# Self attention of a decoder layer on one core: the causal cut of the transposed scores, made by TensorE or by GpSimd

## The chip, the core and the metric

The kernel runs on one core of a Trainium2 chip. The time is that of the whole kernel on the device, in microseconds (us), median of several runs; smaller is better. TensorE (PE) multiplies, with its weight loads listed apart as PEld; VectorE is DVE, ScalarE is ACT, GpSimd is POOL, SyncE (SP) issues the transfers. Each engine works through its own program in order, and the programs meet in semaphores.

## The reference, cut to what matters

One decoder layer on x (4 x 1024 x 512) with a context (4 x 1024 x 512), 16 heads of 32: layer norm and self attention, layer norm and cross attention, layer norm and a two-layer MLP of 2048, each added to its input. Of the self attention:

```python
scores = jnp.einsum('bhqd,bhkd->bhqk', q, kh) / jnp.sqrt(jnp.float32(D))
block_repr = k.reshape(B, nb, BLOCK, D).mean(axis=2)
r = jax.nn.relu(block_repr @ r_w1.T + r_b1) @ r_w2.T + r_b2
keep0 = jax.nn.sigmoid(r[0, :, 0]) > 0.5
allowed = keep0[:, None] & keep0[None, :]
...
scores = jnp.where(allowed_pos[None, None], scores, NEG)
causal = jnp.triu(jnp.ones((S, S), bool), k=1)
scores = jnp.where(causal[None, None], -jnp.inf, scores)
p = jax.nn.softmax(scores, axis=-1)
out = jnp.einsum('bhqk,bhkd->bhqd', p, vh)
```

Every query sees only keys up to its own place, and blocks of 64 keys or queries that a small router drops are pushed to -1e9. All outputs are f32.

## The kernel before, in words

The layer is a chain of stages, each with its own buffers: projections of the context (tag `d_`) and of x (`a_`), self attention (`b_`), projection (`c_`), cross attention (`e_`), projection (`f_`), MLP (`m_`). Self and cross attention are the same function, `attention_stage`; `causal` is true in `b_` alone, and only that stage is touched.

A round n is one group of four heads (HG = 4) of one batch: 16 rounds. In a round the transposed scores (keys down the partitions, queries along the columns) are worked through in twelve steps: k = 0 to 3 for the first half of the 512-query halves (`h` = 0) with key tiles t = 0 to 3, and k = 4 to 11 for the second with t = 0 to 7. `first` is the first query column of a step that any key of its tile may reach: 0, 128, 256, 384 for k = 0 to 3, 0 for k = 4 to 8, then 128, 256, 384 for k = 9 to 11. A step is diagonal when its key tile lies among the queries of its half: k = 0 to 3 and 8 to 11.

TensorE's program (from L1148): in step k, head by head, the scores of step k + 1 (`scores`, L1093, into one of three PSUM banks), matmuls of the scores in their natural layout for the row maxima of the next rounds (`max_scores`, L1063), spread over the steps by a planner (L790 to L820) that counts for each step how much VectorE has to do (`busy`); after head 2 the values' matmuls of step k (`weigh`, L1111), and at the steps named by `sum_at` the sums of a half (`sum_up`, L1122). In `scores` each f32 score matmul of a diagonal step is followed by a second one, of a bf16 identity with `mask_kq`, that adds -1e30 above the diagonal in the first 128 valid columns (L1107). The natural scores have such a mask of their own (L1085).

ScalarE takes the exp of each head's scores into `probs` (L1049), of which there are NF + NR = 5 + 5 buffers of 4 x 512 columns: five in turn for the first step of each group, five for the others. The softmax sums are not taken per step: GpSimd adds the probs of a group's later steps onto those of its first (`add`, L930), and `sum_up` multiplies ones with the first's probs only. `groups` (L757) has three groups: (0, 4), (4, 4), (8, 4), as (first step, number of steps). The add onto a first step waits until `weigh` has read it (L936), since it overwrites it. VectorE copies the values' result out (`copy_outs`, L963) and turns and inverts the sums (`invert`, L987), one or more steps after their cause; GpSimd multiplies both (`normalise`, L942). All these places are counted from `last_step` and `sum_at` (L763).

Of the kernel before, what the change touches and what calls it, by code (L numbers as in the profile page):

```python
# [29 lines left out]
ALU = mybir.AluOpType  # L30
# [6 lines left out]
P = 128  # L37
B, S, D = 4, 1024, 512
H, DH = 16, 32
HG = P // DH  # L40
# [4 lines left out]
TOK = 512  # L45
SUB = TOK // P
HALVES = S // TOK
# [8 lines left out]
ROWS = AUG + 3  # L56
# [684 lines left out]
def attention_stage(nc, tag, ident, q_hi, q_lo, k_hi, k_lo, v, out, keep=None, mask_qk=None,  # L741
                    mask_kq=None, ident_bf=None):
    causal = keep is not None
    N = B * NG
# [4 lines left out]
             for t in range((h + 1) * TOK // P if causal else KT)]  # L749
# [6 lines left out]

    groups = ([(0, 4), (4, 4), (8, 4)] if causal else  # L757
              [(0, 3), (3, 3), (6, 2), (8, 3), (11, 3), (14, 2)])
# [3 lines left out]
    firsts_of = {h: [k for k in firsts if steps[k][0] == h] for h in range(HALVES)}  # L762
    sum_at = {h: last_step[h] + 3 for h in range(HALVES)}  # L763
    VISIT_HEAD = 2
# [28 lines left out]
    for h in range(HALVES):  # L793
        busy[(last_step[h] + 1) % NS] += 0.7
        busy[(sum_at[h] + 1) % NS] += 1.7
# [26 lines left out]
    with ExitStack() as ctx:  # L822
# [18 lines left out]
        consts_set, ones_set = sem("consts_set"), sem("ones_set")  # L841
        added = sem("added")
        loaded = [sem(f"loaded{p}") for p in range(SETS)]
# [11 lines left out]
        with nc.Block() as block:  # L855
# [64 lines left out]
            def _(pool):  # L920
# [7 lines left out]
                pool.wait_ge(consts_set, FILLS * (SETS - 1))  # L928

                def add(n, k):  # L930
                    k0, _ = groups[group_of[k]]
                    before = n * len(rests) + rests.index(k)
                    first = steps[k][2]
                    pool.wait_ge(exped, n * NBLOCKS + (k + 1) * HG)
                    if k == k0 + 1:
                        pool.wait_ge(weighed, n * NS + k0 + 1)  # L936
                    else:
                        pool.wait_ge(added, before)
                    into = probs[:, home(n, k0), :, first:TOK]
                    pool.tensor_tensor(into, into, probs[:, home(n, k), :, first:TOK], ALU.add).then_inc(added, 1)  # L940
# [6 lines left out]
                for n in range(N):  # L947
                    for k in range(NS):
                        for h in range(HALVES):
                            back, at = divmod(sum_at[h] + 3, NS)  # L950
                            if at == k and n >= back:
                                normalise(n - back, h)
                        if k in rests:
                            add(n, k)
# [3 lines left out]
            def _(dve):  # L958
# [47 lines left out]
                for n in range(N):  # L1006
                    for k in range(NS):
                        for h in range(HALVES):
                            back, at = divmod(last_step[h] + 1, NS)
                            if at == k and n >= back:  # L1010
                                copy_outs(n - back, h)
                            back, at = divmod(sum_at[h] + 1, NS)
                            if at == k and n >= back:
                                invert(n - back, h)
# [38 lines left out]
            def _(pe):  # L1053
# [9 lines left out]
                def max_scores(n, u):  # L1063
# [14 lines left out]
                    for bank in range(banks):  # L1078
                        cols = max(width, 256)
                        diagonal = causal and bank == banks - 1  # L1080
                        last = pe.matmul(nat[:, bank_of[u] + bank, 0:cols], qs[p][0:rows, j, t * P:(t + 1) * P],  # L1081
                                         ks[p][0:rows, j, bank * width:bank * width + cols], start=True,
                                         stop=not diagonal)
                        if diagonal:
                            last = pe.matmul(nat[:, bank_of[u] + bank, width - P:width], ident_bf[:], mask_qk[:],  # L1085
                                             start=False, stop=True)
# [6 lines left out]
                def scores(n, k, j):  # L1093
# [3 lines left out]
                    if k == 0 and j == 0:  # L1097
# [3 lines left out]
                    lo = min(first, TOK - 256)  # L1101
                    diagonal = causal and t * P >= h * TOK
                    last = pe.matmul(st_ps[:, bank, lo:TOK], ks[p][0:ROWS, j, t * P:(t + 1) * P],  # L1103
                                     qs[p][0:ROWS, j, h * TOK + lo:(h + 1) * TOK], start=True,
                                     stop=not diagonal)
                    if diagonal:
                        last = pe.matmul(st_ps[:, bank, first:first + P], ident_bf[:], mask_kq[:],  # L1107
                                         start=False, stop=True)
                    last.then_inc(st_ready, 1)

                def weigh(n, k):  # L1111
                    h, t, first = steps[k]
                    pe.wait_ge(exped, n * NBLOCKS + (k + 1) * HG)
                    if t == 0 and n * HALVES + h >= 1:
                        pe.wait_ge(outs_copied, n * HALVES + h)
# [32 lines left out]
                for n in range(N):  # L1148
                    for k in range(NS):
                        for j in range(HG):  # L1150
# [12 lines left out]
                            if j == VISIT_HEAD:  # L1163
                                weigh(n, k)
                                for h in range(HALVES):
                                    back, at = divmod(sum_at[h], NS)
                                    if at == k and n >= back:
                                        sum_up(n - back, h)
                sum_up(N - 1, HALVES - 1)
        sem.clear()  # L1170
# [322 lines left out]
```

## Time and profile before

| | |
|---|---|
| Median of 3 runs | 3414.98 us (3411.88 to 3415.19) |
| Profiled execution | 3417.59 us, span 3415.8 us |
| Mean granted TensorE clock in it | 0.953 |
| TensorE busy | 3130.5 us (92%), 16138 matmuls |
| PEld / VectorE / ScalarE / GpSimd busy | 60% / 52% / 36% / 57% |
| TENSOR_REDUCE of row maxima, L975, `b_` | x512, 364.7 us busy |
| ACTIVATE exp, L1049, `b_` | x768, 350.4 us busy |
| TENSOR_TENSOR adds, L940, `b_` | x144, 446.8 us busy |
| Score matmuls, L1103, `b_` | x768, 299.1 us busy |

The profile is of one execution, by the hardware profiler. Busy is the union of an engine's instructions; matmuls overlap, and their ends are modelled, so the distance from one start to the next says more than a duration. "Idle before, releaser" is how long the engine stood still before an instruction and what ended that. The chain that ended last lies in the MLP stage, since each stage begins when the one before is over; a stage's own time is therefore read from its own stretch.

### The profile page before, as it was taken

The numbers are of one execution on the slowest core, as the hardware profiler recorded it, in microseconds if no ns is written. First come the engines' busy times: TensorE is split into PE (matmuls) and PEld (weight loads), VectorE is DVE, ScalarE is ACT, GpSimd is POOL, SyncE is SP. The second block draws the span as 40 slices with busy tenths as digits, with TensorE's granted clock in tenths as the row PEclk, the third lists the DMA queues.
The fourth block names the chain that finished last, engine by engine and source line by source line (L and its number), as shares of the span: only waits on it lengthen the run. The fifth ranks groups of instructions, "written<-read, shape, count | busy, mean of one in ns | idle before, by whom it ended". The sixth has DMA issues, their size and how long they took to land. (4 is left out here: it accounts for less than half of the span.)

```text
span 3415.8 us, 41706 instructions
## 1 busy us (share of the span) xinstructions
PE 3130.5 (92%) x16138; PEld 2036.1 (60%) x16138; DVE 1772.4 (52%) x2373; ACT 1228.9 (36%) x2305; POOL 1943.8 (57%) x896
## 2 busy tenths in 40 slices
PE   7978997999999986978999999999967599999999
PEld 6867885455555545754444444444346488888887
DVE  4526554666666635758777777777449311111110
ACT  2112220455555552222666666666622211111111
POOL 3114333677777776644888888888866443222232
PEclk9979997999999998996999999999988799999999
DMA  5535546444444405535242424242047521111110
GB/s 203 174 123 173 197 148 162 93 100 100 100 100 100 100 17 179 206 140 129 59 91 59 91 58 92 57 93 54 10 140 282 206 74 50 50 50 50 50 47 15
DMA packets 211604, 360.66 MB, mean 106 GB/s; under 512 B 16312, under 2 KB 92600, under 8 KB 207312
## 3 DMA queue, kind: packets, MB, share of 16 engines
q1 hardware_dynamic: 211408, 358.01, 36.5%
q8 instruction: 127, 2.08, 0.3%
q14 instruction: 69, 0.57, 0.1%
HBM read 214.20 MB, written 142.61 MB: 104 GB/s over the span
## 5 line engine op out<-in xcount | busy, mean ns | idle before, releaser
L940 POOL TENSOR_TENSOR e_probs<-e_probs 128x2048 f32<-128x2048 f32 x160 | 733.4, 4585 | 173.1 <-ACT e_probs L1049 168.4
L1049 ACT ACTIVATE e_probs<-e_st 128x512 f32<-128x512 f32 x1024 | 554.2, 598 | 404.0 <-PE e_st L1103 394.1
L975 DVE TENSOR_REDUCE e_neg_max<-e_nat 128x1 f32<-128x1024 f32 x512 | 602.1, 1218 | 146.3 <-PE e_nat L1081 141.3
L940 POOL TENSOR_TENSOR b_probs<-b_probs 128x1536 f32<-128x1536 f32 (+1 forms) x144 | 446.8, 3103 | 224.3 <-ACT b_probs L1049 214.5
L1049 ACT ACTIVATE b_probs<-b_st 128x512 f32<-128x512 f32 (+3 forms) x768 | 350.4, 490 | 386.2 <-PE b_st L1107 298.3
L975 DVE TENSOR_REDUCE b_neg_max<-b_nat 128x1 f32<-128x128 f32 (+7 forms) x512 | 364.7, 751 | 181.2 <-PE b_nat L1085 178.6
L1301 POOL TENSOR_TENSOR m_hid_lo<-m_hid,m_hid_hi 128x512 fp32r<-128x512 f32 x128 | 165.2, 1290 | 463.2 <-DVE m_hid_hi L1322 463.2
L1103 PE MATMUL e_st<-e_qs,e_ks 99*128 99x512 f32 x1024 | 387.1, 428 | 4.3 <-ACT e_probs L1049 2.9
L1081 PE MATMUL e_nat<-e_ks,e_qs 96*128 96x512 f32 x1024 | 343.2, 424 | 39.5 <-DVE e_neg_max L975 27.9
L1322 DVE CAST m_hid_hi<-m_hid 128x512 fp32r<-128x512 f32 x128 | 58.5, 457 | 600.4 <-ACT m_hid L1274 600.4
L1103 PEld LDWEIGHTS e_st<-e_qs,e_ks 99*128 99x128 f32 x1024 | 174.2, 188 | 257.3 <-ACT e_probs L1049 201.1
L1103 PE MATMUL b_st<-b_qs,b_ks 99*128 99x512 f32 (+2 forms) x768 | 299.1, 432 | 5.0 <-DVE b_turned_sums L994 2.5
L1274 ACT ACTIVATE m_hid<-m_h_ps,m_b 128x512 f32<-128x512 f32 x128 | 88.2, 689 | 593.3 <-PE m_h_ps L113 593.3
L1081 PE MATMUL b_nat<-b_ks,b_qs 97*128 97x384 f32 (+4 forms) x768 | 251.0, 409 | 27.8 <-DMA b_ks<-b_key_mask 19.1
L1117 PE MATMUL e_pv<-e_probs,e_vs 128*32 128x512 f32 x2048 | 273.3, 606 | 0.7 <-ACT e_probs L1049 0.7
L1081 PEld LDWEIGHTS e_nat<-e_ks,e_qs 96*128 96x128 f32 x1024 | 194.5, 199 | 124.6 <-DVE e_neg_max L975 66.2
L1103 PEld LDWEIGHTS b_st<-b_qs,b_ks 99*128 99x128 f32 x768 | 147.5, 199 | 141.2 <-ACT b_probs L1049 89.7
L113 PE MATMUL m_h_ps<-m_x_hi,m_w_hi 128*128 128x512 f32 x512 | 200.9, 392 | 22.2 <-DMA m_x_lo<-xt_lo 20.6
L113 PE MATMUL m_o_ps<-m_w_hi,m_hid_hi 128*128 128x512 f32 x512 | 203.2, 397 | 2.2 <-POOL m_hid_lo L1301 2.2
L113 PE MATMUL m_o_ps<-m_w_hi,m_hid_lo 128*128 128x512 f32 x512 | 203.1, 397 | 0.0
L113 PE MATMUL m_o_ps<-m_w_lo,m_hid_hi 128*128 128x512 f32 x512 | 203.1, 397 | 0.0
L113 PE MATMUL m_h_ps<-m_x_hi,m_w_lo 128*128 128x512 f32 x512 | 201.3, 393 | 0.0
(197 smaller groups left out, 5313.2 us busy)
## 6 DMA issues: line engine op xcount, KB each, us to landing
b_qs<-sq_hi SPq DMA_DIRECT2D x30, 512.0 KB, 6.6
b_ks<-sk_hi SPq DMA_DIRECT2D x30, 512.0 KB, 14.1
e_qs<-cq_hi SPq DMA_DIRECT2D x30, 512.0 KB, 6.7
e_ks<-ck_hi SPq DMA_DIRECT2D x30, 512.0 KB, 14.4
d_x<-in_ctx SPq DMA_DIRECT2D x8, 1024.0 KB, 6.1
ck_hi<-d_part_hi SPq DMA_DIRECT2D x32, 256.0 KB, 6.2
ck_lo<-d_part_lo SPq DMA_DIRECT2D x32, 256.0 KB, 6.1
cv<-d_tok_out SPq DMA_DIRECT2D x32, 256.0 KB, 5.1
```

The source lines that it names most:

```text
L113: last = pe.matmul(out, w, x, start=(start and n == 0 and m == 0), stop=(stop and n == len(pairs) - 1 and m == 2))
L940: pool.tensor_tensor(into, into, probs[:, home(n, k), :, first:TOK], ALU.add).then_inc(added, 1)
L975: dve.tensor_reduce(neg_max[:, u:u + 1], nat[:, bank_of[u]:bank_of[u] + banks, 0:keys // banks], AX.XY, ALU.max, negate=True).then_inc(max ...
L1049: act.activation(probs[:, home(n, k), j, first:TOK], st_ps[:, bank_at("scores", blk), first:TOK], ACT.Exp).then_inc(exped, 1)
L1081: last = pe.matmul(nat[:, bank_of[u] + bank, 0:cols], qs[p][0:rows, j, t * P:(t + 1) * P], ks[p][0:rows, j, bank * width:bank * width + co ...
L1103: last = pe.matmul(st_ps[:, bank, lo:TOK], ks[p][0:ROWS, j, t * P:(t + 1) * P], qs[p][0:ROWS, j, h * TOK + lo:(h + 1) * TOK], start=True, ...
L1117: last = pe.matmul(pv_ps[j * DH:(j + 1) * DH, first:TOK], vs[n % SETS][:, t, j * DH:(j + 1) * DH], probs[:, home(n, k), j, first:TOK], sta ...
L1274: act.activation(hid[:, c % RING, :], h_ps[:, c % RING, :], ACT.Relu, bias=b1_sb[:, c:c + 1]).then_inc(relu_done, 1)
L1301: pool.tensor_tensor(hid_lo[:, c % RING, :], hid[:, c % RING, :], hid_hi[:, c % RING, :].bitcast(F32), ALU.subtract).then_inc(hid_lo_done, 1)
L1322: dve.tensor_copy(hid_hi[:, c % RING, :], hid[:, c % RING, :]).then_inc(hid_hi_done, 1)
```

## The change

Only `attention_stage` is touched, and for cross attention nothing changes. In self attention

- `scores` issues no mask matmul; the score matmul ends its bank alone;
- GpSimd's new `clear(n, k)` runs an `affine_select` in place on the 128 diagonal columns of the four heads' probs of each diagonal step, once the exps of the step are there, and writes 0 where the key lies behind the query; it counts up `cleared`;
- `weigh` and `add` wait for `cleared` on diagonal steps;
- `weigh` is issued a step later (`LATE = 1`), and what is counted from it with it: `sum_at`, `copy_outs`, `invert`, `normalise`, and the planner's `busy`; the last weighing of the stage stands behind the loop;
- group (4, 4) becomes (4, 2) and (6, 2): step 6 is a first step, so its probs are not added onto others, and the sums of the second half run over three groups of four matmuls.

The natural scores keep their masks. The rest is a change of a name.

```diff
--- before.py
+++ after.py
@@ -754,13 +754,16 @@
 
 
 
-    groups = ([(0, 4), (4, 4), (8, 4)] if causal else
+    groups = ([(0, 4), (4, 2), (6, 2), (8, 4)] if causal else
               [(0, 3), (3, 3), (6, 2), (8, 3), (11, 3), (14, 2)])
     firsts = [k for k, _ in groups]
     rests = [k for k in range(NS) if k not in firsts]
     group_of = [max(g for g, k0 in enumerate(firsts) if k0 <= k) for k in range(NS)]
     firsts_of = {h: [k for k in firsts if steps[k][0] == h] for h in range(HALVES)}
-    sum_at = {h: last_step[h] + 3 for h in range(HALVES)}
+
+    LATE = 1 if causal else 0
+    diagonal = [causal and t * P >= h * TOK for h, t, _ in steps]
+    sum_at = {h: last_step[h] + LATE + 3 for h in range(HALVES)}
     VISIT_HEAD = 2
 
 
@@ -791,7 +794,7 @@
     busy = [0.0] * NS
     busy[TURN] += 0.6
     for h in range(HALVES):
-        busy[(last_step[h] + 1) % NS] += 0.7
+        busy[(last_step[h] + LATE + 1) % NS] += 0.7
         busy[(sum_at[h] + 1) % NS] += 1.7
     free = []
     for at in range(NBLOCKS):
@@ -839,7 +842,7 @@
         pv_ps = ctx.enter_context(nc.psum_tensor(tag + "pv", [P, 512], F32))
 
         consts_set, ones_set = sem("consts_set"), sem("ones_set")
-        added = sem("added")
+        added, cleared = sem("added"), sem("cleared")
         loaded = [sem(f"loaded{p}") for p in range(SETS)]
         rows_loaded = [sem(f"rows_loaded{p}") for p in range(SETS)]
         nat_ready, maxed, max_turned, max_split = sem("nat_ready"), sem("maxed"), sem("max_turned"), sem("max_split")
@@ -927,11 +930,19 @@
                     pool.memset(qs[p][AUG:ROWS].bitcast(F32), 0.0).then_inc(consts_set, 1)
                 pool.wait_ge(consts_set, FILLS * (SETS - 1))
 
+                def clear(n, k):
+                    cut = probs[:, home(n, k), :, steps[k][2]:steps[k][2] + P]
+                    pool.wait_ge(exped, n * NBLOCKS + (k + 1) * HG)
+                    pool.affine_select(out=cut, in_=cut, compare_op=ALU.is_ge, fill=0.0, base=0,
+                                       pattern=[[0, HG], [1, P]], channel_multiplier=-1).then_inc(cleared, 1)
+
                 def add(n, k):
                     k0, _ = groups[group_of[k]]
                     before = n * len(rests) + rests.index(k)
                     first = steps[k][2]
                     pool.wait_ge(exped, n * NBLOCKS + (k + 1) * HG)
+                    if diagonal[k]:
+                        pool.wait_ge(cleared, n * sum(diagonal) + sum(diagonal[:k + 1]))
                     if k == k0 + 1:
                         pool.wait_ge(weighed, n * NS + k0 + 1)
                     else:
@@ -950,6 +961,8 @@
                             back, at = divmod(sum_at[h] + 3, NS)
                             if at == k and n >= back:
                                 normalise(n - back, h)
+                        if diagonal[k]:
+                            clear(n, k)
                         if k in rests:
                             add(n, k)
                 normalise(N - 1, HALVES - 1)
@@ -1006,7 +1019,7 @@
                 for n in range(N):
                     for k in range(NS):
                         for h in range(HALVES):
-                            back, at = divmod(last_step[h] + 1, NS)
+                            back, at = divmod(last_step[h] + LATE + 1, NS)
                             if at == k and n >= back:
                                 copy_outs(n - back, h)
                             back, at = divmod(sum_at[h] + 1, NS)
@@ -1077,11 +1090,11 @@
                         pe.wait_ge(maxed, n * UNITS + u + 1 - reach[u])
                     for bank in range(banks):
                         cols = max(width, 256)
-                        diagonal = causal and bank == banks - 1
+                        cut = causal and bank == banks - 1
                         last = pe.matmul(nat[:, bank_of[u] + bank, 0:cols], qs[p][0:rows, j, t * P:(t + 1) * P],
                                          ks[p][0:rows, j, bank * width:bank * width + cols], start=True,
-                                         stop=not diagonal)
-                        if diagonal:
+                                         stop=not cut)
+                        if cut:
                             last = pe.matmul(nat[:, bank_of[u] + bank, width - P:width], ident_bf[:], mask_qk[:],
                                              start=False, stop=True)
                     last.then_inc(nat_ready, 1)
@@ -1099,18 +1112,15 @@
                     bank_free("scores", blk)
                     bank = bank_at("scores", blk)
                     lo = min(first, TOK - 256)
-                    diagonal = causal and t * P >= h * TOK
-                    last = pe.matmul(st_ps[:, bank, lo:TOK], ks[p][0:ROWS, j, t * P:(t + 1) * P],
-                                     qs[p][0:ROWS, j, h * TOK + lo:(h + 1) * TOK], start=True,
-                                     stop=not diagonal)
-                    if diagonal:
-                        last = pe.matmul(st_ps[:, bank, first:first + P], ident_bf[:], mask_kq[:],
-                                         start=False, stop=True)
-                    last.then_inc(st_ready, 1)
+                    pe.matmul(st_ps[:, bank, lo:TOK], ks[p][0:ROWS, j, t * P:(t + 1) * P],
+                              qs[p][0:ROWS, j, h * TOK + lo:(h + 1) * TOK], start=True,
+                              stop=True).then_inc(st_ready, 1)
 
                 def weigh(n, k):
                     h, t, first = steps[k]
                     pe.wait_ge(exped, n * NBLOCKS + (k + 1) * HG)
+                    if diagonal[k]:
+                        pe.wait_ge(cleared, n * sum(diagonal) + sum(diagonal[:k + 1]))
                     if t == 0 and n * HALVES + h >= 1:
                         pe.wait_ge(outs_copied, n * HALVES + h)
                     for j in range(HG):
@@ -1161,11 +1171,14 @@
                                 for u in later_units[k][j]:
                                     max_scores(n + 2, u)
                             if j == VISIT_HEAD:
-                                weigh(n, k)
+                                if n * NS + k >= LATE:
+                                    weigh(*divmod(n * NS + k - LATE, NS))
                                 for h in range(HALVES):
                                     back, at = divmod(sum_at[h], NS)
                                     if at == k and n >= back:
                                         sum_up(n - back, h)
+                for k in range(NS - LATE, NS):
+                    weigh(N - 1, k)
                 sum_up(N - 1, HALVES - 1)
         sem.clear()
```

## Rows read from the trace of the kernel before

**Rows 1.** Busy time of each engine in stretches of self attention (instructions in brackets).

```profile
core 0: us, PE busy (x) PEld busy (x) DVE busy (x) ACT busy (x) POOL busy (x), PEclk, DMA share, GB/s
1030.00:1115.00 85.00, 81.97 (x563) 42.79 (x562) 55.73 (x85) 43.80 (x97) 60.85 (x22) 1.00 0.46 100
775.00:860.00 85.00, 81.61 (x560) 42.53 (x559) 55.71 (x84) 43.24 (x96) 60.85 (x22) 1.00 0.46 100
901.35:943.92 42.57, 41.05 (x283) 21.44 (x282) 27.94 (x43) 21.97 (x49) 30.43 (x12) 1.00 0.47 100
```

**Rows 2.** Timeline, TensorE at the stage's end: start, length, instruction, count.

```profile
1281.69 3.64 PE L1129 MATMUL b_st<-b_probs,b_ones 128*32 128x512 f32 x16 [6.79 <-POOL b_probs L940]
```

**Rows 3.** Timeline, TensorE: score matmuls with masks, then the values'.

```profile
900.83 0.23 PE L1107 MATMUL b_st<-mask_kq,ident_bf 128*128 128x128 bf16 x1
900.87 0.48 PE L1103 MATMUL b_st<-b_qs,b_ks 99*128 99x512 f32 x1
901.19 0.23 PE L1107 MATMUL b_st<-mask_kq,ident_bf 128*128 128x128 bf16 x1
901.35 0.43 PE L1117 MATMUL b_pv<-b_probs,b_vs 128*32 128x128 f32 x8
```

**Rows 4.** Timeline, TensorE: f32 matmuls behind an f32 matmul and behind a mask.

```profile
917.35 0.48 PE L1103 MATMUL b_st<-b_qs,b_ks 99*128 99x512 f32 x1
917.76 1.06 PE L1117 MATMUL b_pv<-b_probs,b_vs 128*32 128x512 f32 x8
918.76 0.73 PE L1103 MATMUL b_st<-b_qs,b_ks 99*128 99x512 f32 x2
919.32 0.28 PE L1081 MATMUL b_nat<-b_ks,b_qs 97*128 97x256 f32 x1
919.45 0.23 PE L1085 MATMUL b_nat<-mask_qk,ident_bf 128*128 128x128 bf16 x1
919.49 0.36 PE L1081 MATMUL b_nat<-b_ks,b_qs 97*128 97x256 f32 x1
919.69 0.23 PE L1085 MATMUL b_nat<-mask_qk,ident_bf 128*128 128x128 bf16 x1
```

**Rows 5.** Timeline, TensorE: the two sums of a round, and a wait behind one.

```profile
911.75 1.90 PE L1129 MATMUL b_st<-b_probs,b_ones 128*32 128x512 f32 x16
913.58 0.39 PE L1103 MATMUL b_st<-b_qs,b_ks 99*128 99x256 f32 x1
...
913.85 0.47 PE L1103 MATMUL b_st<-b_qs,b_ks 99*128 99x512 f32 x1
914.49 0.73 PE L1103 MATMUL b_st<-b_qs,b_ks 99*128 99x512 f32 x2 [0.17 <-DVE b_turned_sums L994]
...
926.57 1.04 PE L1129 MATMUL b_st<-b_probs,b_ones 128*32 128x512 f32 x8
927.54 0.73 PE L1103 MATMUL b_st<-b_qs,b_ks 99*128 99x512 f32 x2
```

**Rows 6.** Groups of GpSimd's instructions: count, busy us, mean ns, idle before.

```profile
L940 POOL TENSOR_TENSOR b_probs<-b_probs 128x2048 f32<-128x2048 f32 x48 | 219.5, 4572 | 51.6 <-ACT b_probs L1049 47.0
L940 POOL TENSOR_TENSOR b_probs<-b_probs 128x1536 f32<-128x1536 f32 x32 | 110.5, 3454 | 146.6 <-ACT b_probs L1049 146.6
L945 POOL TENSOR_TENSOR b_outs<-b_outs,b_turned_sums 128x512 f32<-128x512 f32 x32 | 41.3, 1291 | 5.6 <-DVE b_turned_sums L998 5.6
L926 POOL MEMSET b_ks<- 3x4096 f32 x2 | 7.0, 3508 | 0.0
```

**Rows 7.** Timeline, GpSimd at the kernel's start: two of its four selects.

```profile
1.60 0.29 POOL L1407 TENSOR_SCALAR_AFFINE_SELECT ident<-ident 128x128 f32<-128x128 f32 x1 [0.25 <-POOL mask_kq L1404]
1.85 0.29 POOL L1407 TENSOR_SCALAR_AFFINE_SELECT ident_bf<-ident_bf 128x128 bf16<-128x128 bf16 x1
```

**Rows 8.** Timeline, TensorE: values' matmuls of steps 1, 3, 8, 9 and 11.

```profile
908.48 0.85 PE L1117 MATMUL b_pv<-b_probs,b_vs 128*32 128x384 f32 x8
915.15 0.43 PE L1117 MATMUL b_pv<-b_probs,b_vs 128*32 128x128 f32 x8
934.50 1.06 PE L1117 MATMUL b_pv<-b_probs,b_vs 128*32 128x512 f32 x8
938.38 0.85 PE L1117 MATMUL b_pv<-b_probs,b_vs 128*32 128x384 f32 x8
943.92 0.42 PE L1117 MATMUL b_pv<-b_probs,b_vs 128*32 128x128 f32 x8
```

**Rows 9.** Timeline, TensorE: the longest wait of a round.

```profile
938.17 0.28 PE L1091 MATMUL b_nat<-ident,b_neg_max 128*32 128x128 f32 x1 [0.83 <-DVE b_neg_max L975]
```

## What the change should do to the time, worked out before it was run

> **What bounds the kernel now.** I read the busy time of each engine by stretches first. Of the change only the self attention stage is touched: in the steady part of its loop TensorE is busy 81.6 to 82.0 of 85 us at the full granted clock, while GpSimd is busy 60.9, VectorE 55.7 and ScalarE 43 to 44 [rows 1]. One round (one group of four heads, twelve steps of four heads) takes 42.57 us, and TensorE works in 41.05 of them. So TensorE's own program order sets the time, and what counts is the distance from the start of one matmul to the start of the next. Two things must be asked: how much of that distance goes away, and which instruction of TensorE then waits for GpSimd. In the last round there are no row maxima left to work out, and there GpSimd is the bound: the last group sums wait 6.79 us for it [rows 2].
>
> **The sums on TensorE, per round.** A score matmul is followed by its mask matmul on the eight diagonal steps (k = 0 to 3 and 8 to 11), four heads each: 32 masks a round, 512 in all. I read starts. The mask itself holds the next matmul up by only 0.04 us (900.83 to 900.87), but the matmul after a mask starts its successor later than it would after another f32 matmul: 256 columns take 0.13 us after an f32 matmul (919.32 to 919.45) and 0.20 after a mask (919.49 to 919.69) [rows 3, 4]. A removed mask with an f32 matmul behind it thus saves 0.04 + 0.07 = 0.11 to 0.12 us. Before the values' matmuls, score and mask take 0.32 + 0.16 = 0.48 us, a score alone 0.41 (917.35 to 917.76) [rows 3, 4]: 0.07 saved. 24 of the first kind and 8 of the second give 24 x 0.115 + 8 x 0.07 = 3.3 us.
>
> The fourth group of sums adds four f32 matmuls of 512 columns side by side, once a round: two groups take 1.83 us, one 0.97 [rows 5], so 0.86 more. The sums of the second half move from step 2 to step 3 of the next round, away from where a score now waits for the transpose that frees their bank (0.17 us idle; start to start 0.64 instead of 0.34): 0.3 back. Nothing else of TensorE's order is new: the values' matmuls are the same, one step later, behind the same number of scores. Without any new wait a round saves 3.3 - 0.86 + 0.3 = 2.8 us.
>
> **GpSimd, per round.** Gone is the add of step 6, 4.57 us [rows 6]. New are eight clears of 128 x (4 x 128). The load is no trouble: 30.4 us now [rows 1], about 31.5 then. The price C of a clear is not in the trace. The nearest rows are the four selects of 128 x 128 at the start of the kernel: 0.29 us each, starts 0.25 apart [rows 7]. Low end: their 0.25 and for 384 more elements the slope of a memset (4096 elements in 3.51 us, 0.86 ns an element) [rows 6]: 0.25 + 0.33 = 0.58 us. High end: four times 0.295, 1.18 us; the two-input operation of 512 elements takes 1.29 [rows 6]. I take 0.70, near the low end, because the select reads one operand as the memset row does in writing, and the two-input row pays for a second. The Trainium skill, GPSIMD Engine Reference, section Performance pitfalls for Q7 kernels, has compare-then-select bodies at 2.03 cycles an element, and 1.03 when unrolled twice; at its 1.2 GHz that would be an estimate of 0.87 or 0.44 us for 512 elements before the fixed part, and the total below would be about 2 or 13 us less than before; no row here says which body the select has.
>
> **The new wait.** The weighing of step k (the values' matmuls) waits for the clear of k. GpSimd works in order, and ahead of some clears stands an add that itself can only start when the weighing of the group's first step is over, since the add writes on those probabilities (L936). With the weighing a step later that release comes a step later too. I number TensorE's places by the step at which they stand; the weighing at place p is that of step p - 1.
>
> Place 9 to 11: at place 9 the values of step 8 are weighed, 1.0 us; about 0.1 us later the add of step 9 starts, 3.45 us, then the normalising product that now stands at step 10, 1.29, then the clear of step 10: 5.84 + C after place 9. TensorE needs the clear at place 11. Place 9 to 11 takes 943.92 - 938.38 = 5.54 us now [rows 8]; 0.4 more since two wider weighings stand between, 0.8 less for the eight masks in it: 5.1. The stall is 0.7 + C, 1.4 us with C = 0.70.
>
> Place 1 to 3: the weighing of step 0, then the add of step 1 and the clear of step 2: 1.0 + 0.1 + 3.45 + C = 4.55 + C. TensorE takes 915.15 - 908.48 = 6.67 us now [rows 8]; less 1.83 for the sums that move behind place 3 and 0.3 for the wait behind them [rows 5], less 0.5 for five masks, 0.5 more for wider weighings, and about 0.5 more for one row maximum that the planner moves from step 4 to step 3 (its sum_at entry moves): 5.0. The stall is C - 0.4, 0.3 us. The clears of steps 3, 8, 9, 11 and 0, by the same count, come before they are needed, that of step 11 by under half a microsecond.
>
> What else moves stays covered. The first-of-group probs take four of five buffers a round instead of three; the exp of step 6 now waits for the sums of the second half of the round before, which stand two steps (some 8 us) ahead of it; without that cover ScalarE, and behind it the scores, would stand still for what is missing. SyncE's load of the round after next waits for the last weighing of the round before, a step later, and has most of a round left. The copy, the inverse and the normalising product each move by a step along with what they wait for.
>
> What waits behind a stalled weighing is all of TensorE's queue: scores, row maxima, and through them ScalarE and VectorE; nothing of it is got back, since TensorE is the bound. Where it stands still for 0.83 us in each round already, its granted clock stays at 1.00 [rows 1, 9], the 2.4 GHz level; I expect that with 1.4 too.
>
> **The sum.** A round: 2.8 - 1.4 - 0.3 = 1.1 us saved, or in general 2.5 - 2C. Fourteen rounds have all their row maxima: 15 us. At the ends some comes back: the values' matmuls begin one step late (2 us), the last two rounds hang on GpSimd rather than on the masks (eight clears against one add, 8 x 0.7 - 4.57 = 1 us, with the adds waiting for later weighings another 2), and the third group in the last sums runs at the lower clock, where two take 3.64 us against 1.90 in mid-stage [rows 2, 5]: some 1 us beyond the masks' saving there. Together 6. Result: 9 us less. On the profiled run (3417.6 us, span 3415.8) that is 3408.6, on the median of the runs shown 3415.0 - 9 = 3406 us, which is what I forecast. With C = 0.58 it is 3402, with C = 0.80 3409; gain and loss balance at C near 1.04.
>
> **The rivals.**
> Slow clears: at C = 1.18 the two stalls leave 14 x 0.14 = 2 us of gain, 6 us at the ends are lost, and the clears of steps 11 and 0 come late as well, since their slack of some 0.4 us is gone, by up to 0.9 a round: 3419 to 3432. It decides from C = 1.04. For it: four separate runs of 128 elements in each partition. Against it: the 0.25 us of 128 must hold some fixed part. Chance 0.24, a third of it within 0.2%.
> The mask is only its 0.04: if the f32 score behind a removed mask keeps its 0.20, a round saves 1.3 - 0.86 + 0.3 = 0.7 and stalls about 1.1 (TensorE arrives later): 0.4 lost a round, 6 at the ends, 3427. Against it stand the two 256-column rows of [rows 4]. Chance 0.08.
> No stalls: if GpSimd is at place 11 in time, a round keeps 2.8 and the kernel ends near 3415 - 39 + 6 = 3382. Against it: the order of GpSimd's program and the 3.45 us row. Chance 0.05.
> The forecast itself has 0.63: 0.41 of it lies beyond 0.2%, and 0.22 within (C from 0.80 to 1.04, or masks worth a little less).
>
> **Chances and range.** 0.2%, 6.8 us, is about what a measurement tells here. Faster 0.41 + 0.05 = 0.46; same 0.22 + 0.08 = 0.30; slower 0.16 + 0.08 = 0.24. The range goes from 3392 (C = 0.58, masks worth a bit more, cheap ends) to 3430.
>
> **What would show it.** In the profile after, no matmul writes scores from the mask; score matmuls of 256 columns stand 0.13 us apart where nothing holds them; TensorE waits for the clears 14 to 16 times for about 1.4 us each before the 256-column weighing at place 11 and shorter before that at place 3; clears last 0.6 to 0.8 us; the sums of the second half take 2.7 us. A round is 41.3 to 41.6 us long. The forecast falls if clears last over a microsecond, if the stalls sit elsewhere, or if the granted clock dips within a round.

## The result and the profile after

The changed kernel takes 3450.2 us, median of four runs (3441.0 to 3459.4), against 3415.1 us before (3411.9 to 3415.4): 1.0105 of the time, 95% interval 1.0075 to 1.0135. I had forecast 3406 us, range 3392 to 3430. It became slower by 35 us where I expected 9 us less. The profiled execution is the slowest of the four, 3459.4 us with a span of 3457.7; the time before scatters over 3.5 us, that after over 18.

The first view, the busy time by stretches, already holds the answer. These rows of after stand against [rows 1]; columns as there.

```profile
core 0: us, PE busy (x) PEld busy (x) DVE busy (x) ACT busy (x) POOL busy (x), PEclk, DMA share, GB/s
600.00:1290.00 690.00, 641.32 (x3858) 325.82 (x3860) 412.53 (x622) 331.59 (x736) 464.44 (x274) 0.88 0.39 86
...
818.25:863.64 45.39, 42.41 (x258) 21.75 (x258) 27.84 (x42) 21.77 (x48) 30.61 (x18) 0.89 0.43 94
863.64:913.46 49.82, 46.96 (x257) 23.49 (x257) 27.93 (x42) 21.80 (x48) 30.59 (x18) 0.79 0.39 86
1000.94:1042.65 41.71, 38.06 (x257) 19.41 (x258) 27.28 (x42) 21.75 (x48) 30.67 (x18) 1.00 0.46 102
1042.65:1084.38 41.73, 38.09 (x257) 19.42 (x257) 27.28 (x42) 21.76 (x48) 30.66 (x18) 1.00 0.46 102
```

The last four stretches are one round each, from one matmul that turns the row maxima (now L1104) to the next. All four hold the same work: 257 or 258 matmuls, 48 exps, 18 operations of GpSimd. Two have a granted clock of 1.00 and take 41.7 us, 0.85 less than the 42.57 before; two have 0.89 and 0.79 and take 45.4 and 49.8. From 600 to 1290 us the granted clock is 0.88; before it was 0.98 there, below 1.00 only at the two ends of the loop.

What TensorE does where the clock falls, and where it does not (timeline of after; start, length, instruction, idle before and its releaser):

```profile
1049.57 0.64 PE L1127 MATMUL b_pv<-b_probs,b_vs 128*32 128x256 f32 x8 [1.58 <-POOL b_probs L936]
1050.14 0.68 PE L1115 MATMUL b_st<-b_qs,b_ks 99*128 99x512 f32 x2
...
870.56 0.99 PE L1127 MATMUL b_pv<-b_probs,b_vs 128*32 128x256 f32 x8 [1.58 <-POOL b_probs L936]
871.48 1.12 PE L1115 MATMUL b_st<-b_qs,b_ks 99*128 99x512 f32 x2
872.39 0.84 PE L1094 MATMUL b_nat<-b_ks,b_qs 97*128 97x384 f32 x2
873.04 0.33 PE L1098 MATMUL b_nat<-mask_qk,ident_bf 128*128 128x128 bf16 x1
...
913.46 0.28 PE L1104 MATMUL b_nat<-ident,b_neg_max 128*32 128x128 f32 x1 [1.01 <-DVE b_neg_max L988]
```

Both weighings are those of step 10 at place 11. Both waited 1.58 us for the clear (L936). Behind the first a pair of 512-column scores takes 0.68 us, behind the second 1.12: from there TensorE runs at its lower level, 1.2 GHz, for 10 to 20 us. Such a fall comes in 11 of the 15 round-to-round distances of the profiled run, each time within 2 us behind the end of this wait (ten waits of 1.58 us and one of 1.34). In the other four the wait was 0.76, 1.05 and twice 1.58 us: it can pass without a fall. Some 6 us earlier TensorE waits 1.01 us for the last row maximum, 0.83 before [rows 9]; it waits 1.01 us also where only the masks are gone (e8 below).

GpSimd and its new instruction, in a round at the full clock (timeline of after):

```profile
1044.14 3.47 POOL L951 TENSOR_TENSOR b_probs<-b_probs 128x1536 f32<-128x1536 f32 x1 [1.75 <-PE b_pv L1127]
1047.56 1.28 POOL L956 TENSOR_TENSOR b_outs<-b_outs,b_turned_sums 128x512 f32<-128x512 f32 x1
1048.77 0.65 POOL L936 TENSOR_SCALAR_AFFINE_SELECT b_probs<-b_probs 128x512 f32<-128x512 f32 x1
```

All its clears between 600 and 1300 us (group of instructions; columns as in [rows 6]):

```profile
L936 POOL TENSOR_SCALAR_AFFINE_SELECT b_probs<-b_probs 128x512 f32<-128x512 f32 x124 | 78.4, 639 | 56.2 <-ACT b_probs L1062 55.8
```

This is the chain that I had worked out for place 11: the add of step 9, released by the weighing of step 8, the normalising product, the clear. The clear takes 0.64 us.

The other stall, at place 3, is one for which the profile names the wrong releaser (timeline of after):

```profile
1015.07 3.47 POOL L951 TENSOR_TENSOR b_probs<-b_probs 128x1536 f32<-128x1536 f32 x1 [1.51 <-PE b_pv L1127]
1018.50 0.63 POOL L936 TENSOR_SCALAR_AFFINE_SELECT b_probs<-b_probs 128x512 f32<-128x512 f32 x1
...
1019.28 0.64 PE L1127 MATMUL b_pv<-b_probs,b_vs 128*32 128x256 f32 x8 [0.49 <-ACT b_probs L1062]
```

The exps of that step are older; the clear ends at 1019.13, and 0.15 us later the weighing starts, the same distance as at place 11 (1049.42 to 1049.57). Without clears this wait is not there (e3 below).

### The profile page after: what moved, and what is told of

It reads as the page before. It is cut to its first block and busy times, and to the rows that moved or that the text cites. A ratio compares the mean times of both kernels' runs of the same rounds, so it can differ in the third digit from the quotient of the medians.

```text
span 3457.7 us, 41149 instructions
## 1 busy us (share of the span) xinstructions
PE 3148.6 (91%) x15754; PEld 2036.2 (59%) x15754; DVE 1772.4 (51%) x2373; ACT 1224.5 (35%) x2305; POOL 1946.9 (56%) x1008
## 5 line engine op out<-in xcount | busy, mean ns | idle before, releaser
L951 POOL TENSOR_TENSOR b_probs<-b_probs 128x1536 f32<-128x1536 f32 (+3 forms) x128 | 374.3, 2924 | 205.2 <-PE b_pv L1127 196.1
L1314 POOL TENSOR_TENSOR m_hid_lo<-m_hid,m_hid_hi 128x512 fp32r<-128x512 f32 x128 | 165.1, 1290 | 463.4 <-DVE m_hid_hi L1335 463.4
L1094 PE MATMUL b_nat<-b_ks,b_qs 97*128 97x384 f32 (+4 forms) x768 | 260.2, 424 | 25.0 <-DMA b_ks<-b_key_mask 19.2
L1127 PE MATMUL b_pv<-b_probs,b_vs 128*32 128x512 f32 (+3 forms) x1536 | 184.0, 554 | 33.5 <-POOL b_probs L936 30.4
```

The lines of the kernel that those rows point to most:

```text
L1127: last = pe.matmul(pv_ps[j * DH:(j + 1) * DH, first:TOK], vs[n % SETS][:, t, j * DH:(j + 1) * DH], probs[:, home(n, k), j, first:TOK], sta ...
L1314: pool.tensor_tensor(hid_lo[:, c % RING, :], hid[:, c % RING, :], hid_hi[:, c % RING, :].bitcast(F32), ALU.subtract).then_inc(hid_lo_done, 1)
```

## The experiments

Two theories for the lower clock. A: it falls because TensorE stands still for the clear, as long as it does. B: it falls because the mask matmuls' work is gone from TensorE. Rounds are counted from one turning matmul to the next, in the profiled run of each kernel. A "fall" is a stretch at 1.2 GHz that begins within these fifteen distances. The low stretch in which every loop starts is not counted: it ends between 604 and 631 us, why so differently is not shown, and the first distance is 40 to 50 us long. Where rounds are given, the first is left out.

**e1, the normalising product a step earlier.**

```diff
-                            back, at = divmod(sum_at[h] + 3, NS)
+                            back, at = divmod(sum_at[h] + 2, NS)
```

> The changed kernel with one edit: GpSimd's normalising product is issued a step earlier, so that at step 10 it no longer stands between the add of step 9 and the clear of step 10. All results are computed. In the changed kernel rounds at the full clock last 41.7 us and rounds with a fall of the granted clock 45 to 50. Theory A, the clock falls because TensorE stands still (1.0 to 1.6 us for the clear of step 10, shortly after 1.0 us for the row maxima): that stall shrinks by 1.29 us to about 0.1, the clock holds, rounds take about 40.5 us and the kernel about 3385. Theory B, the clock falls because the mask matmuls' work is gone from TensorE: the clock falls as often as before, some rounds still take over 44 us, and the kernel takes 3420 to 3440.

Measured: 3392.3 us (3388.7 to 3395.3), 0.9923 of before (0.9907 to 0.9939). Rounds of 40.5 us, all alike after the first, no fall. Busy time in a stretch of it, and its weighing at place 11:

```profile
1030.00:1115.00 85.00, 79.92 (x536) 40.61 (x535) 57.65 (x87) 45.73 (x100) 65.42 (x37) 1.00 0.49 107
```

```profile
1089.82 0.64 PE L1127 MATMUL b_pv<-b_probs,b_vs 128*32 128x256 f32 x8 [0.36 <-POOL b_probs L936]
```

The wait at place 11 went from 1.58 to 0.36 us, and the clock is at 1.00. One number is changed in the source, and 58 us lie between the two medians: 1.2 us a round is the shorter wait, 18 us in 15 rounds, and some 40 are left for the clock. For A, against B.

**e2, every clear ahead of the add of the step before.**

```diff
                         if diagonal[k]:
                             clear(n, k)
-                        if k in rests:
-                            add(n, k)
+                        m, i = divmod(n * NS + k - 1, NS)
+                        if m >= 0 and i in rests:
+                            add(m, i)
+                add(N - 1, NS - 1)
                 normalise(N - 1, HALVES - 1)
```

> The changed kernel with the adds issued one step later in GpSimd's program, so that each clear stands ahead of the add of the step before it and behind no add that waits for a weighing. All results are computed. Theory A: no weighing waits for a clear, the clock holds at 1.00 in the steady part, rounds take 39.5 to 40.0 us, the kernel 3372 to 3382. Theory B: no stall either, but the clock still falls in most rounds, and the kernel takes 3410 to 3430.

Measured: 3375.5 us (3374.5 to 3380.7), 0.9878 (0.9859 to 0.9897). Rounds of 39.5 us (two of 39.9 and 40.2), no fall. TensorE's waits between 700 and 1190 us, summed (us, times, longest):

```profile
PE b_nat L1106 <- DVE b_neg_max L990: 12.2, 12, 1.0
PE b_nat L1096 <- DVE b_neg_max L990: 6.7, 25, 0.3
PE b_st L1117 <- DMA b_qs<-b_max_lo: 0.4, 1, 0.4
```

No weighing waits any more. The adds did not need to go first: GpSimd has time for both.

**e3, no clears and no waits for them.** The edit takes `clear`'s call and the two waits on `cleared` out of the changed kernel.

> The changed kernel without the clears and without the waits for them; probabilities above the diagonal stay in, so this part of the computation is left out. It shows what the masks' removal, the late weighing and the fourth group give together with GpSimd out of the way: rounds of 39.5 to 39.9 us at the full clock (42.57 less 2.8) by both theories. Theory A: the clock holds, about 3370 to 3378. Theory B: it falls in most rounds, over 3400.

Measured: 3376.2 us (two runs, 3372.3 and 3380.2), 0.9876 (0.9851 to 0.9902); rounds of 39.5 us, apart from a few of up to 40.1, no fall. This kernel leaves the causal cut of the transposed scores out, so it serves as a measure only. With e2 it says that well-placed clears cost nothing that these runs could show, and that the masks may go without the clock falling: B is out.

**e4, masks back and a stall as before.**

```diff
+                    done = n * sum(diagonal) + sum(diagonal[:k])
+                    if done:
+                        pool.wait_ge(filled, done)
+                    pool.memset(filler[:], 0.0).then_inc(filled, 1)
                     pool.affine_select(out=cut, in_=cut, compare_op=ALU.is_ge, fill=0.0, base=0,
...
+                    if diagonal[k]:
+                        last = pe.matmul(st_ps[:, bank, first:first + P], ident_bf[:], mask_kq[:],
+                                         start=False, stop=True)
```

> The changed kernel with the mask matmuls put back after the scores (the clears then change nothing), and a memset of 760 elements to a spare buffer ahead of every clear, about 0.7 us each, so that the weighing at place 11 still waits more than 1 us for its clear. All results are computed. Full-clock rounds should take about 44.5 us by both theories (42.57, 0.9 for the fourth group, 1.3 to 1.9 of stalls, less 0.3 to 0.6 for the later weighing). Theory A: the clock falls as in the changed kernel, in half of the rounds or more, over 3475. Theory B: the masks keep TensorE active enough, the clock holds, 3450 to 3465.

Measured: 3516.8 us (two runs, 3498.2 and 3535.4), 1.029 (1.022 to 1.035). Rounds without a fall take 44.8 us, seven of fifteen have one and take 48.9 to 53.0. The wait at place 11 is 1.35 to 1.37 us in all rounds but the first, with a fall behind it or without. The weighing at place 11, and the busy time of a stretch:

```profile
1071.62 0.64 PE L1136 MATMUL b_pv<-b_probs,b_vs 128*32 128x256 f32 x8 [1.35 <-POOL b_probs L941]
```

```profile
1115.00:1200.00 85.00, 80.14 (x519) 42.20 (x522) 49.66 (x76) 39.99 (x87) 64.26 (x47) 0.92 0.46 101
```

All masks are back and the clock falls, with a wait of 1.35 us at place 11. With e1 to e3 the question between A and B is closed.

**e5, e2 with the three old groups.**

```diff
-    groups = ([(0, 4), (4, 2), (6, 2), (8, 4)] if causal else
+    groups = ([(0, 4), (4, 4), (8, 4)] if causal else
```

> The kernel of e2_clears_first with the three groups of the kernel before: GpSimd adds step 6 again (4.58 us a round) and TensorE sums two groups in the second half instead of three. All results are computed. e2 took rounds of 39.5 us, GpSimd busy 32.7 of 42.5. If TensorE alone sets the time there, the round loses the fourth group's 0.86 us: 38.6 to 38.8, the kernel 3360 to 3366. If GpSimd, then busy about 36 of 38.7 us with adds that wait for weighings, gets in the way, weighings wait for clears again, the clock may fall, and it takes 3375 or more.

Measured: 3363.9 us (3361.7 to 3373.8), 0.9847 (0.9827 to 0.9868), the fastest of all. Rounds of 38.6 to 38.7 us, no fall. Busy time in a stretch:

```profile
1030.00:1115.00 85.00, 81.86 (x561) 41.63 (x560) 59.18 (x92) 47.52 (x107) 77.00 (x44) 1.00 0.55 120
```

GpSimd is busy 77.0 of 85 us, and still TensorE hardly waits for it: between 700 and 1190 us its listed waits for ScalarE sum to 2.4 us, and none for GpSimd is listed. Once the clears stand first, the fourth group relieves an engine that does not need it. The round is 0.88 us shorter without it.

**e6 and e7, the parts that keep the masks.** e6 is the kernel before with `LATE = 1` alone; e7 is e6 with the fourth group.

> The kernel before with the weighing, and what is counted from it, one step later, and nothing else of the change: masks on TensorE, three groups, no clears. All results are computed. My sum gave the later sums 0.3 us a round, since a score no longer waits for the transpose behind them: rounds of 42.0 to 42.3 us, 3405 to 3413. A rival: the later weighing costs as much elsewhere, 3415 to 3420.

Measured: 3404.8 us (3404.5 to 3405.7), 0.9958 (0.9944 to 0.9973), rounds of 41.9 us.

> The kernel of e6 with the fourth group of sums: masks on TensorE, no clears. All results are computed. The step from e6 is the group's price: 0.86 us a round and 1 us more at the cold end, 15 us in all, so 3420 to 3428. The step from here to e3_no_clears (3376) is then the 512 masks: at 0.115 and 0.07 us each 53 us; at 0.04 each it would have been 20.

Measured: 3416.5 us (ten runs, 3412.7 to 3422.7), 0.9989 (0.9978 to 1.0000), rounds of 42.7 us. So the later weighing gives 0.70 us a round (42.57 to 41.87), over twice my figure, and the fourth group costs 0.87 a round and 12 us in all. From here to e3 the masks go: 42.74 to 39.53, 3.2 us a round. The two medians lie 40 us apart, less than fifteen times 3.2 and than the 53 that I expected; 4.8 us of that is the first distance of e3's profiled run, 49.6 us against 44.8, with its longer low stretch.

**e8, the masks off alone.** The kernel before without the second matmul in `scores`.

> The kernel before without the mask matmuls of the transposed scores and nothing put in their place: probabilities above the diagonal stay in, that part of the computation is left out. If a mask costs 0.115 us where an f32 matmul follows and 0.07 ahead of the values, rounds take 42.57 - 3.3 = 39.2 to 39.4 us at a granted clock of 1.00 and the kernel 3365 to 3372. If it costs only its own 0.04, 41.3 us and 3395. Were TensorE's clock to fall for want of the masks' work, rounds of over 42 us would appear.

Measured: 3375.5 us (two runs, 3375.3 and 3375.7), 0.9872 (0.9853 to 0.9892), rounds of 39.8 us, no fall in them. That is less than I expected of it: 2.8 us a round and not 3.3, 0.4 less than between e7 and e3: in this kernel a score still waits for the transpose behind the sums (3.5 us in 12 times). This kernel too leaves the cut out. The price of a removed mask lies at 0.09 to 0.10 us, far from the 0.04 of the rival.

**e9 and e11, a stall elsewhere.** Both are e2 with a wait of TensorE for the add of step 5, in a stretch of 512-column matmuls: in e9 behind the weighing at step 6, in e11 ahead of it.

```diff
+                                if causal and k == 6:
+                                    pe.wait_ge(added, n * len(rests) + rests.index(5) + 1)
```

> The kernel of e2_clears_first with one wait more: behind the weighing at step 6, TensorE waits until GpSimd has done the add of step 5. By the trace that is about 1.0 us of standstill, as long as the wait for the clear of step 10 in the changed kernel, but seven to eight us after the last narrow step, in the stretch of 512-column matmuls. All results are computed. Theory A1, any standstill of about 1 us in a round lets the granted clock fall: falls in half of the rounds or more, as in the changed kernel, 3420 or more. Theory A2, it takes the wait where it stood, behind 1.0 us of waiting for row maxima and among the narrow steps: the clock holds, rounds take 40.5 to 40.7 us, the kernel 3390 to 3396.

Measured: 3391.3 us (two runs, 3388.9 and 3393.8), 0.9927 (0.9898 to 0.9956). Rounds of 40.1 to 40.3, no fall. But the stall was 0.58 us, not 1.0, so it could not tell the places apart; hence e11, where `weigh` holds the same wait for k = 5:

> The kernel of e9 with its extra wait ahead of the weighing at step 6 instead of behind it. In e9 TensorE stood still for 0.58 us there and the clock held; the weighing of 1.0 us in front filled the rest. Now the standstill should be 1.5 to 1.6 us, the same as at place 11 in the changed kernel (1.58), but 512-column matmuls stand on both sides. All results are computed. Theory A1, a standstill of 1.6 us lets the clock fall wherever it is: stretches at 1.2 GHz in most rounds, rounds of 45 us, 3440 or more. Theory A2, the place matters (narrow steps and 1.0 us of waiting for row maxima just before): the clock holds, rounds of 41.1 us, the kernel 3400 to 3406.

Measured: 3450.0 us (five runs, 3439.7 to 3450.7), 1.0080 (1.0055 to 1.0104). The weighing at step 6 with the scores behind it, and the busy time of a stretch of one round's length:

```profile
893.13 1.06 PE L1131 MATMUL b_pv<-b_probs,b_vs 128*32 128x512 f32 x8 [1.64 <-POOL b_probs L951]
894.13 0.95 PE L1117 MATMUL b_st<-b_qs,b_ks 99*128 99x512 f32 x2
```

```profile
850.00:894.30 44.30, 41.08 (x258) 20.40 (x257) 27.51 (x42) 21.77 (x48) 30.48 (x18) 0.92 0.44 96
```

A standstill of 1.64 us among wide matmuls; twelve of fifteen distances have a fall, each 6.8 us long, and these rounds take 44.3 to 44.5 us against 41.2 to 41.6 without. So the place does not protect (A1). The falls are shorter here than behind place 11, where they lasted 10 to 20 us; what sets their length is not shown.

**e10, clears first, weighing not late.** e2 with `LATE = 0`.

> The kernel of e2_clears_first with the weighing back at its own step (LATE = 0). All results are computed. The clear of a step then starts only when its exps are done and must be over before the weighing of the same step: by my reading the weighings of steps 9 and 11 wait 1.3 to 1.9 us each, rounds take 43 us at the full clock, and with such waits the clock falls: 3440 or more. If it holds, 3435 to 3440. If the later weighing is not needed at all once the clears stand first, 3375 to 3380.

Measured: 3483.7 us (two runs, 3480.2 and 3487.1), 1.020 (1.017 to 1.023). Rounds of 43.6 us without a fall and 48.4 to 48.8 with one, nearly every second. TensorE's waits for clears between 700 and 1190 us (us, times, longest), and the two kinds of round (timeline of e10, at 742 us a round without a fall, at 778 us one with):

```profile
PE b_pv L1129 <- POOL b_probs L936: 21.0, 15, 1.8
```

```profile
742.14 0.42 PE L1129 MATMUL b_pv<-b_probs,b_vs 128*32 128x128 f32 x8 [1.76 <-POOL b_probs L936]
...
777.78 0.28 PE L1106 MATMUL b_nat<-ident,b_neg_max 128*32 128x128 f32 x1 [1.02 <-DVE b_neg_max L990]
779.27 1.51 PE L1129 MATMUL b_pv<-b_probs,b_vs 128*32 128x384 f32 x8 [1.21 <-POOL b_probs L936]
```

The wait of 1.76 us stands only in the six rounds without a fall, and no fall begins in the 30 us behind it. In the eight rounds with one, the fall begins within 2 us of the turning matmul: behind the 1.0 us for the row maxima, and seven times inside the wait of 1.2 us for a clear that follows after 0.3 us of work. So two shorter waits close together do it as well, and the longest single wait is not the measure of it. A ninth fall, of 3.4 us, begins in the first distance, 1.5 us behind a wait of 2.19 us. With the clears the later weighing is needed, as the change has it, even when they stand first.

**e12, half the stall.** e1 with a memset of 380 elements ahead of the clear of step 10.

> The kernel of e1_norm_early with a memset of 380 elements to a spare buffer ahead of the clear of step 10, some 0.35 us, so that the wait at place 11 grows from 0.35 to 0.7 us, halfway to the 1.58 of the changed kernel. All results are computed. If the clock's fall needs about what the changed kernel has, it holds: rounds of 40.9 us, 3396 to 3402. If it is on the edge already, falls appear in some rounds, which then take 43 us or more, and the kernel 3405 to 3430.

Measured: 3395.8 us (five runs, 3394.5 to 3405.8), 0.9932 (0.9911 to 0.9954), rounds of 40.8 to 40.9 us, no fall. Its weighing at place 11:

```profile
1058.77 0.64 PE L1132 MATMUL b_pv<-b_probs,b_vs 128*32 128x256 f32 x8 [0.69 <-POOL b_probs L941]
```

All kernels by their longest wait for GpSimd behind the first distance; the wait of 0.8 to 1.0 us for the row maxima is in each of them:

| kernel | longest wait for GpSimd, us | distances with a fall | round without, us | us |
|---|---|---|---|---|
| before | none | 0 | 42.6 | 3415 to 3420 |
| e2, e3, e5 | none | 0 | 39.5, 39.5, 38.6 | 3375, 3376, 3364 |
| e1 | 0.36 | 0 | 40.5 | 3392 |
| e9 | 0.58 | 0 | 40.2 | 3391 |
| e12 | 0.7 | 0 | 40.8 | 3396 |
| e4 | 1.35 | 7 of 15 | 44.8 | 3517 |
| the change | 1.58 (one round 1.05, one 1.34) | 11 of 15 | 41.7 | 3450 |
| e11 | 1.64 | 12 of 15 | 41.2 | 3450 |
| e10 | 1.76, with no fall behind it; the falls come at 1.0 and 1.2 with 0.3 of work between | 9 of 15 | 43.6 | 3484 |

The waiting of a whole round would part the kernels too: all waits of 0.15 us and more add up to 2.8 us at most in the rounds of those without a fall, and to 3.2 to 4.8 in the full-clock rounds of those with falls. No run holds that sum still while the waits are spread out. What speaks for waits within a few microseconds is the moment: in the changed kernel, e4 and e11 every fall begins within 2 us behind the long wait.

## Why the prediction was wrong, step by step

- **What bounds.** Right: TensorE's order sets the round, and the stage's end hangs on GpSimd.
- **The masks, 3.3 us a round.** Right: 3.2 (e7 to e3), and in e2 one 256-column score starts the next matmul 0.12 us later, though the first behind a weighing 0.22.
- **The fourth group, 0.86.** Right: 0.87.
- **The later weighing, 0.3.** Too small: 0.70 (e6). Together a round without stalls saves 3.04 us (42.57 to 39.53), not 2.8.
- **The price of a clear, 0.70, bounds 0.58 and 1.18.** Measured 0.64. The nearest row was that of the small selects, plus a slope from a memset; that held. From one run of 128 elements to four, 0.35 us for 384 elements more, is 0.91 ns an element, near the memset's 0.86. The rival of slow clears is out. The totals of 2 and 13 us less that stand beside 0.87 and 0.44 us do not follow from the prediction's own formula, which gives 5 and 17 at those prices; the forecast did not use them.
- **The two stalls.** Both are where I put them. With C = 0.64 my sums give 1.34 and 0.24; measured are 1.58 and 0.49. Each is short by 0.25: I had allowed 0.1 us from the end of the weighing to the add, where the trace has 0.21, and nothing from the clear to the weighing, where it has 0.15.
- **The sum at the full clock.** 41.7 us a round, where I had 41.3 to 41.6. The fifteen distances of the profiled run add up to 678.2 us; at 41.72 each they would be 625.8. By this the falls cost 52 us in that run. 3459.4 - 52.4 = 3407.0 us is my estimate of the same run without them, and my figure on that scale was 3408.6. That the two are so close is partly luck: a round saves 0.85 us and not 1.1, 12 us in fourteen rounds and not 15, and the ends cost correspondingly less than my 6.
- **The step that failed** is half a sentence: of the standstill of 0.83 us, behind which the granted clock stays at 1.00, it says "I expect that with 1.4 too". I carried one harmless wait over to one twice as long. No row of before bears on 1.4 us in mid-stage; the row nearest to it was a warning: behind 6.79 us of waiting the sums ran at half speed [rows 2, 5]. Between 0.83 and 6.79 us the effect had no bound, and I gave it neither a term nor a rival, only a word among the signs of being wrong. What the runs showed in its place: behind a wait of 1.58 us the clock fell in ten of twelve rounds, and a stretch at the lower level costs 0.36 to 0.46 of its length in this kernel, e4 and e11 (in e11 6.8 us of it made the round 3.1 us longer, in the changed kernel 20.5 us of it 8.1). The 52 us of the profiled run are more than any other term of the sum; the masks are worth 48 in fifteen rounds.
- **The rivals.** None of them was it. The one of no stalls, with 3382 us, had the mechanism right for e2: with the clears out of the way 3375.
- **The clears' place.** I worked out the stall of place 11 from an order on GpSimd that holds a product of 1.28 us between an add and a clear, and took that order as given. It was the cheapest thing to change: e1 moves it, e2 does away with both stalls.

The Trainium skill has in TensorE: Matmul & The Clock Gate, section HAM oscillation, the same failure: a loop whose waits recur lets the clock drop once per pass. The case agrees in kind: 11 of 15 rounds, 0.88 granted on average. The waits in the page's example, 3 to 5 us, are longer than the 1.34 to 1.64 us that were enough here, and for this kernel the measurement decides. I had not weighed that section.

What stays open: why a wait of 1.58 us passed in two rounds and not in ten, one of 1.64 in three of fifteen (e11), one of 1.35 in seven of fourteen (e4) and one of 1.76 in all six (e10); where above 0.7 us the effect begins (1.05 us passed once, 1.34 did not); and over what stretch neighbouring waits add up. That the run-to-run spread of the changed kernel (18 us) comes from the number of falls is likely (mean granted clock 0.931, 0.934, 0.936, 0.937 in the order of falling times), but the rounds of the other three runs were not read.

## What to carry to other kernels

A recurring wait on TensorE has two prices, the wait itself and, from some length on, the clock behind it; here 1.6 us of waiting cost 1.6 us in some rounds and 5 to 10 in others. When a change adds a wait longer than any that the loop has, or puts one close to another, give the clock a term and a rival of its own, priced from any stretch of the trace at the lower level. And when an in-order engine takes on a short job that another engine waits for, put it ahead of the long jobs that wait themselves: that alone turned 3450 us into 3375.

## What the runs showed of the hardware that I had not expected

A wait of 1.35, 1.58 or 1.64 us, once in a round of 41 to 45 us, brought TensorE's granted clock down to 1.2 GHz in 7, 11 and 12 of fifteen distances, although it was busy for some nine tenths of the time; waits of 1.0 and 1.2 us with 0.3 us of work between did so in eight; 0.36, 0.58 and 0.7 us, each with a second wait of 1.0 us in the round, did not in any of fifteen distances each. A bf16 mask matmul of 128 columns behind an f32 matmul costs 0.09 to 0.10 us and not the 0.04 from its start to the next. A select in place over four runs of 128 elements takes 0.64 us on GpSimd, little more than twice that over one run (0.29).
